# A Mamba and mixture-of-experts layer in fp32: another layout of the tile table, the last five blocks combined in tiles that lie idle, and an order of its own for the last post stage

## What is computed

```python
xz = einsum('bld,ed->ble', layernorm(x), in_proj_w);  x_ssm, z = split(xz, 2)
x_conv = silu(conv4(x_ssm) + conv_b)                  # causal, 4 taps
B, C, delta = split(einsum(x_conv, x_proj_w))         # 16, 16, 1 (softplus)
h = exp(delta * A) * h + delta * B * x_conv           # over time, 16 states
y = (sum_n(h * C) + D_param * x_conv) * silu(z)
x1 = x + einsum(y, out_proj_w)
top 2 of 8 experts by softmax(router(layernorm(x1))), weights w
out = x1 + sum_k w_k * (layernorm(x1) @ expert_weights[top_k])
```

## Time and profile before

| | us |
|---|---|
| median of 3 runs | 2971.43 |
| the runs | 2971.4 to 2974.65 |
| profiled execution | 2975.89 |
| its span, first to last instruction | 2974.1 |
| TensorE / VectorE / GpSimd / ScalarE busy | 2415.0 / 2278.7 / 1811.8 / 1486.8 |
| mean granted TensorE clock, share of full | 0.875 |

### The profile page before, as it was taken

How to read it: one execution, slowest core, us unless ns; L and a number is a source line. 1 busy time by engine, 2 the same in 40 slices (tenths; PEclk the granted TensorE clock), 3 DMA queues, 4 the chain that set the end, 5 groups by cost and what they waited for, 6 DMA issues and landing times.

```text
span 2974.1 us, 34543 instructions
## 1 busy us (share of the span) xinstructions
PE 2415.0 (81%) x9510; PEld 1401.4 (47%) x9510; DVE 2278.7 (77%) x3189; ACT 1486.8 (50%) x2417; POOL 1811.8 (61%) x1420
## 2 busy tenths in 40 slices
PE   5668686798979898898979898898979898887754
PEld 2335353455545554555545554545545554444421
DVE  3889888898888888888888898888888888665100
ACT  3454545465555556455655546465645556342210
POOL 2455766566566767576676767577675767574412
PEclk8778777798989999898989898899979898899977
DMA  3762411223233434334343434344343434455735
GB/s 123 243 244 92 142 54 57 85 86 117 72 113 105 144 103 125 116 108 141 108 122 106 139 111 133 105 119 130 115 126 98 150 103 131 124 161 157 192 97 129
DMA packets 192570, 366.27 MB, mean 123 GB/s; under 512 B 22912, under 2 KB 22912, under 8 KB 192384
## 3 DMA queue, kind: packets, MB, share of 16 engines
q1 hardware_dynamic: 144272, 263.26, 27.4%
q0 software_dynamic: 28672, 67.13, 10.6%
q10 hardware_dynamic: 19440, 33.69, 3.1%
HBM read 212.73 MB, written 151.26 MB: 122 GB/s over the span
## 4 chain that ended last, share of the span: by engine, by line
PE 47%; DVE 19%; issue 13%; ACT 7%; DMA 7%; POOL 6%; SPq 0%; DVEq 0%; POOLq 0%; ACTq 0%
PE work L1094 34%; DVE h L919 8%; PE hT L1099 7%; DVE acc L927 6%; PE work L1099 3%; POOL u L646 3%; DMA x_out<-result_scratch,rows_of 3%; PE work L1154 2%; ACT decay L783 2%; DVE xc L950 1%; DMA b_ring<-b_scratch 1%; DMA xe<-row_scratch 1%; ACT L783 1%; POOL x_out L750 1%; DMA result_scratch<-ye 1%
## 5 line engine op out<-in xcount | busy, mean ns | idle before, releaser
L646 POOL TENSOR_TENSOR u<-xc,b_ring 128x1024 f32<-128x1024 f32 x512 | 1229.8, 2411 | 757.2 <-DVE h L919 576.0
L783 ACT ACTIVATE decay<-dt,neg_a 128x512 f32<-128x512 f32 x1024 | 700.8, 689 | 690.1 <-DVE h L919 675.0
L1099 PE MATMUL hT<-ident,h 128*128 128x128 f32 x4096 | 693.4, 305 | 364.6 <-DVE acc L927 290.4
L1099 PEld LDWEIGHTS hT<-ident,h 128*128 128x128 f32 x4096 | 524.7, 156 | 650.3 <-DVE acc L927 285.5
L1094 PE MATMUL work<-w_exp,xeT 128*128 x1528 | 749.1, 636 | 37.4 <-DVE dt L962 13.6
L927 DVE SCALAR_TENSOR_TENSOR acc<-hT,ct,acc 128x512 f32<-128x512 f32 x960 | 699.8, 729 | 86.9 <-PE hT L1099 83.9
L919 DVE TENSOR_TENSOR_SCAN h<-decay,h_last,u 128x512 f32<-128x512 f32 x512 | 652.7, 1275 | 114.1 <-ACT decay L783 77.8
L919 DVE TENSOR_TENSOR_SCAN h<-decay,u 128x512 f32<-128x512 f32 x512 | 621.4, 1215 | 123.6 <-ACT decay L783 93.2
L1094 PE MATMUL work<-xnT,w_in 128*128 128x512 f32 x1024 | 484.2, 618 | 2.2 <-DVE dt L962 1.5
L1094 PEld LDWEIGHTS work<-w_exp,xeT 128*128 128x128 f32 x1528 | 295.5, 204 | 366.8 <-issue 366.1
L750 POOL DMA_INDIRECT x_out<-result_scratch,rows_of x120 | 192.7, 1606 | 184.9 <-DMA x_out<-x_scratch 91.0
(11 more groups left out here) (145 smaller groups left out, 1856.7 us busy)
## 6 DMA issues: line engine op xcount, KB each, us to landing
b_ring<-b_scratch SPq DMA_DIRECT2D x256, 256.0 KB
xe<-row_scratch SPq DMA_DIRECT2D x165, 256.0 KB
result_scratch<-ye SPq DMA_DIRECT2D x165, 256.0 KB
row_scratch<-x_out ACTq DMA_DIRECT2D x32, 1024.0 KB, 4.8
x<-in_x SPq DMA_DIRECT2D x66, 256.0 KB, 5.4
x_scratch<-x SPq DMA_DIRECT2D x64, 256.0 KB, 2.0
xn<-in_x SPq DMA_DIRECT2D x62, 256.0 KB, 3.4
x_out<-x_scratch SPq DMA_DIRECT2D x60, 256.0 KB, 3.1
```

The costliest lines, as they stand in the source:

```text
L646: nc.gpsimd.tensor_tensor(out=u[:, at:at + 2, :], in0=xc[:, half, 2 * k:2 * k + 2, :], in1=b_ring[:, n % ROWS:n % ROWS + 1, :].to_broadcas ...
L783: nc.scalar.activation(decay_bank[g % 2][:], dt[:, half, :], ACT.Exp, scale=neg_a[:, c, n:n + 1]).then_inc(decay_ready, 1)
L1099: last = nc.tensor.transpose(ps[:, k * P:(k + 1) * P], tile(k), ident[:])
```

## The change

Four things. The table of tiles lies with one tile per partition, its numbers in units of rows, which makes `new_group` 14 dependent operations instead of 19, each on few elements. Blocks 11 to 15 ("late", of = 0 to 4) are no longer combined through `x_out` but each in four tiles of its own, by then unused: in `xnT`, the two halves of `h`, `u` and `x1`; their first gathers are issued for all four quarters, then the second ones. Block 11 goes in stage 15, 12 and 13 in the last stage, 14 at the head of the closing tiles, 15 at the end. The results' scratch has three parts instead of two, and the table of group 7 is made at the end of stage 15 instead of in the last stage. The post stage of block 15 has an order of its own (`POST_END`), in which its four weighted first rows go into the idle `xc`. And all tables of places have new numbers, of which two lines are shown; `gate_weights` computes the mask of the ranks first.

```diff
-    COMBINE_PLAN = {j: [j - 5] for j in range(5, BLOCKS - 1)}
-    COMBINE_PLAN[BLOCKS - 1] = [BLOCKS - 6, BLOCKS - 5]
-    COMBINE_PLAN[BLOCKS] = [BLOCKS - 4, BLOCKS - 3]
-    COMBINE_PLAN[BLOCKS + 1] = [BLOCKS - 2]
-    COMBINE_PLAN[BLOCKS + 2] = [BLOCKS - 1]
-    NEW_GROUP = {first + n + 1: g for g, (first, n) in enumerate(GROUPS)}
+    COMBINE_PLAN = {j: j - 5 for j in range(5, BLOCKS)}
+    LATE = 5
+    NEW_GROUP = {first + n + 1: g for g, (first, n) in enumerate(GROUPS[:-2])}
...
-        "silu_z": [60.57],
+        "silu_z": [63.09],
...
-        "expert": [11.51, 14.24, 18.5, 27.8, 31.94, 35.21, 40.91, 44.16, 51.51, 56.71, 58.7, 61.45],
+        "expert": [12.95, 13.84, 18.76, 27.8, 33.76, 34.9, 40.91, 47.46, 52.88, 56.98, 59.44, 64.58],
...
+        if j == BLOCKS - 1:
+            steps += late_in("far", 0) + [(COMBINE_LATE["middle_new_group"][0], ("new_group", len(GROUPS) - 2))]
+        if j == BLOCKS:
+            steps += late_in("mid", 1) + late_in("near", 2)
...
         if j == BLOCKS + 2:
-            return ([("gather", q, 0) for q in range(Q)] + [("gather", q, 1) for q in range(Q)] + [("store", q) for q in range(Q)])
+            return late("late_gather", 4) + late("late_store", 4)
         count = EXPERT_PLAN[j][2]
-        tiles = [[("rows_load", 0), ("rows_load", 1), ("rows_T", 0), ("rows_load", 2), ("rows_evict", 0)]]
+        steps = [("new_group", len(GROUPS) - 1), ("rows_load", 0), ("rows_load", 1)] + late("late_fetch", 4) + late("late_fetch", 3) + late("late_gather", 3)
+        steps += [("rows_T", 0), ("rows_load", 2), ("rows_evict", 0)]
         for i in range(count):
...
-        rows = [[("fetch", q), ("gather", q, 0), ("gather", q, 1), ("store", q)] for q in range(Q)] + [[("fetch_last", q) for q in range(Q)]]
...
-            steps += rows[i // 3] if i % 3 == 0 and i // 3 < len(rows) else []
+            steps += late("late_store", 3) if i == count // 2 else []
...
+        def late_tile(of, q):
+            return (xnT[:, q, :], h[:, 0, q, :], h[:, 1, q, :], u[:, q, :], x1[:, q, :])[of]
+
+        def x_first_of(r, q):
+            return xc[:, 0, q, :] if r == BLOCKS - 1 else x_first[:]
...
+                        if k == 0:
+                            pool.wait_ge(late_loaded[of], 16 * Q)
                         else:
-                            pool.wait_ge(loaded, 16 * (BLOCKS + 1))
+                            pool.wait_ge(late_row[of * Q + q], 16)
...
-                        link(nc.vector.tensor_tensor(out=past, in0=tiles_to[0:1, :].rearrange("p (a e) -> p a e", a=1).to_broadcast([1, XT, E]),
-                                                     in1=tile_no[:].rearrange("p (i a) -> p i a", a=1).to_broadcast([1, XT, E]), op=ALU.is_le))
-                        link(nc.vector.tensor_reduce(expert_f[:], past, AX.X, ALU.add))
+                        link(nc.vector.tensor_scalar(past[:, 0, :], tiles_to[:], tile_at[:, 0:1], None, ALU.is_le))
+                        link(nc.vector.scalar_tensor_tensor(out=past[:, 1, :], in0=tiles_to[:], scalar=tile_at[:, 0:1], in1=tiles_f[:],
+                                                            op0=ALU.is_le, op1=ALU.mult))
+                        link(nc.vector.tensor_reduce(passed[:], past[:], AX.X, ALU.add))
```

More of the change, by code:

```diff
@@ L83, in mamba_moe_kernel @@
-        "gate_exp": [31.68],
-        "gate_sum": [30.88],
-        "gate_weights": [37.97],
-        "rank": [40.13],
-        "row_of": [40.34],
-        "weigh": [41.91, 46.9, 52.3, 57.15],
-        "scatter": [45.9, 48.02, 55.57, 61.9],
+        "load_res": [0, 4.56, 7.16, 13.35],
+        "y_T": [3.95, 4.16, 4.17, 4.17],
+        "y_skip": [5.28, 5.98, 8.38, 9.52],
+        "y_gate": [8.46, 11.27, 11.48, 11.76],
+        "out_project": [10.41, 12.16, 14.54, 16.54],
+        "residual": [14.16, 16.46, 17.58, 18.56],
@@ new lines, in mamba_moe_kernel @@
+        "rstd2": [19.44, 20.88],
+        "store_x1": [12.83, 15.36, 19.16, 19.72],
+        "norm2": [18.08, 18.74, 23.3, 24.11],
+        "norm2_T": [17.86, 18.75, 22.5, 25.68],
+        "norm2_evict": [18.84, 21.17, 25.24, 27.48],
+        "router": [18.55, 19.8, 25.56, 27.11],
+        "gate_logits": [18.75, 22.45, 27.07, 29.84],
+        "gate_top": [32.08],
+        "gate_exp": [34.84],
+        "gate_sum": [33.53],
+        "gate_weights": [37.11],
+        "rank": [39.92],
+        "row_of": [40.66],
@@ L139, in mamba_moe_kernel @@
     }
     PAIRS = [(i, k) for i in range(Q) for k in range(TOP)]
-    INDEX = {"gather": PAIRS, "conv": [(c, k) for c in range(C) for k in range(EDGE)]}
+    INDEX = {"gather": PAIRS, "late": [(i, k) for k in range(TOP) for i in range(Q)], "conv": [(c, k) for c in range(C) for k in range(EDGE)]}
     def steps_in(stage):
@@ L163, in experts_in, with late_in @@
                 for i, at in enumerate(places) if i < EXPERT_PLAN[j][2]]
-    def combine_in(j):
-        blocks = len(COMBINE_PLAN.get(j, []))
-        return [((at + i * N * C) / blocks, (kind, i * Q + s[0]) + tuple(s[1:])) for i in range(blocks) for at, (kind, *s) in steps_in(COMBINE)]
+    def late_in(kind, of):
+        places = COMBINE_LATE[kind + "_fetch"], COMBINE_LATE[kind + "_gather"], COMBINE_LATE[kind + "_store"]
+        return ([(at, ("late_fetch", of, q)) for q, at in enumerate(places[0])] +
+                [(at, ("late_gather", of) + index) for index, at in zip(INDEX["late"], places[1])] +
+                [(at, ("late_store", of, q)) for q, at in enumerate(places[2])])
@@ L179, in closing_steps @@
-        for i, tile in enumerate(tiles):
-            steps += tile
-            steps += rows[i // 3] if i % 3 == 0 and i // 3 < len(rows) else []
+            steps += [("rows_T", i + 1)] * (i + 1 < count) + [("rows_load", i + 3)] * (i + 3 < count)
+            steps += [("rows_evict", i + 1)] * (i + 1 < count) + [("expert", i), ("expert_evict", i), ("rows_store", i)]
+            steps += late("late_store", 3) if i == count // 2 else []
         return steps
@@ L579, in steps_of @@
                     elif s[0] == "store":
[L580 removed]
+                        block, q = COMBINE_PLAN[j], s[1]
                         first = block * T + q * P
[L582 to L587 removed]
+                        sync.wait_ge(gathered[q % 2], 16 * TOP * (2 * block + q // 2 + 1))
@@ L1056, in steps_of @@
-                        if g >= 3:
-                            for k in range(2):
-                                dve.wait_ge(gathered[k], 16 * TOP * Q // 2 * GROUPS[g - 2][0])
-                        link(nc.vector.tensor_copy(rows_of[g % 3][:], result_f[:]))
+                        link(nc.vector.tensor_reduce(result_f[:], token_shift[:], AX.X, ALU.add))
+                        wait_combined(dve, g - 3)
+                        link(nc.vector.tensor_tensor(out=rows_of[g % 3][:], in0=result_f[:], in1=row_f32[:], op=ALU.add))
@@ L1084, in _ @@
         def _(pe):
-            pe.wait_ge(const_step, 16)
+            pe.wait_ge(const_step, 14)
             def take(j, key):
```

322 lines of the change are left out of this document (184 added, 138 removed).

## The result

The changed kernel takes 2882.96 us, the median of four runs (2881.6 to 2892.7), against 2971.41 (2970.8 to 2974.7). The ratio is 0.9694, 95% interval 0.9668 to 0.972, a change of -88.5 us. The forecast was 2881 in 2845 to 2915. The sum was met; two of its terms were met by what offset inside them, as the rest shows.

What follows compares the result with a forecast made beforehand. The prediction looked first at what keeps TensorE waiting in the 272 us tail, then at the scan stages. Terms -47 - 26 - 4 - 13 + 17 - 17 = -90 us gave 2886 against the profiled 2975.9, 2881 for the median, range 2845 to 2915.

Steps and rivals of the forecast that it cites:

- Closing tiles, -47: Closing tiles after the last stage: no store waits among the tile loads any more, 70 us against 117.1.
- the last of the forecast's rivals: Closing tiles: closing gathers slow the tile loads, so TensorE waits as often as before; near 2925 us, chance 0.02.
- Last stage, -26: Last stage, up to the landing of the last scatter and the first closing load: four savings, sum -25.7 us.
- (a): Last stage: group 7's table is made at the end of stage 15, so TensorE's 10.3 us first-tile wait goes.
- (c): End of last stage: the last `weigh` waits for no scatter, no gather stands among the scatters; 4.2 against 6, -1.8 us.
- (d): Last stage to closing tiles: the tile load waits for scatters alone, -7.9 us.
- (b): Last stage: about five of nine TensorE eviction waits go (3.7 us), and the clock is not lowered (about 2 us).
- The third rival: Last stage gets no shorter: a `weigh` waiting for gate weights holds up evictions; 17.8 us given back, 2899, chance 0.10.
- Table, -13: Table in scan stages 3 to 15: 14 operations, 3.1 us instead of 5.0; -1.85 in each of seven stages, wholly on path.
- Seam, +17: Between scan stages: silu behind the last decay, late product after odd stages; +14 odd, +3 even, bounds 0 and +45.
- Rest of the scan stages, -17: Scan stages: 9 us from VectorE's waits for `u`, 8 from the ranks, nothing from the residual; bounds -60 and +40.
- The first rival: Scan stages gain more: half of VectorE's 43.9 us residual wait goes, seam costs nothing; 2842 us, chance 0.15.

## Why the forecast was right, and where it wasn't

**Closing tiles, -47:** -49.7 measured, and +50 when the order is put back. No wait there is over 6.3 us, so the gathers did not slow the loads as the last of the forecast's rivals had it. The fetch burst that was costed at 3 us costs 1.0, and the gathers' 2 don't show. But this is cover, not a low price: with an earlier start the burst costs 5.2 us and the low clock behind it. The forecast took bytes over a rate; the load waits for a queue of issues and transfers in front of it (the issues of the eight fetches alone take 3.7 us).

**Last stage, -26:** -20.5. (a) 10.3: 9.5 by the medians and 10.2 by the traces came back in its experiment, with a table that is 1.7 us shorter. (c) 1.8: from the last product at 2779.88 to the last scatter's end at 2784.33 are 4.45 us, forecast 4.2. (d) 7.9: from the last scatter's issue to the first load are 3.6 us instead of 13.5, 9.9. (b), 3.7 and 2, failed: the eviction waits stayed, and TensorE is busy 94.4 us for 93.2. I had counted places where other transposes stand ahead of the product; in the last tiles nothing but its own do, and it waits 0.88 us for their eviction, where it waited 0.93 and 0.97 before. Hence the last scatter is issued 106.6 us behind the last scan and not 98. The third rival (nothing of (a) to (c)) is refuted: the first weigh step waits 0.74 us for the gate weights. It is the other way round: the later weigh steps stand behind evictions, up to 2780, and an early place for them brought the last scatter forward by 12.5 us.

**Table, -13:** -1.65 each instead of -1.85, seven times -11.6. TensorE's wait shows all of it, as said; the stage lengths of its experiment do so in their sum alone.

**Seam, +17:** the waits at place 0 grew by 41 us in stages 3 to 14 and those at place 61 went (-20): +21. The size was nearly right. The step that failed is the sentence that this part "speaks against the change": with the silu back the kernel is 23 us slower, and with the product back none faster.

**Rest of the scan stages, -17:** the table takes 9.9 of the 14.4 us in stages 3 to 14, so seam and rest together gave -4.5 in the profiles (forecast 0), and -11.6 by the run with the old places. In these stages that run differs from the kernel before by the table, the order of the mask's operations and the results' scratch in three parts with its waits, yet gained 2.8 us where the table gives 9.9; how much of this is one execution's scatter stays open. Inside the term most steps failed: the `u` waits rose by 35 us instead of falling by 9. Only 5.3 of their 14.4 us stood behind a seam, at place 4, where the forecast's reason applies, and these went; at places 38 and 54 they grew from 9 to 47 us. That the later places of B rows and gathers did this is argued, no run moves them alone; the residual's 43.9 us, taken as nothing, went. The ranks' came as said (18.1 to 8.1 with the fill's, forecast -8). What the new numbers visibly bring is TensorE's clock at places 28 to 48, for which the forecast had no term, though the trace before shows it (0.90 in stage 9).

**The first rival** (scan stages gain 39 more) is refuted, and so are the second and the fourth: the seam cost 21 us, not 45 or 112.

So the total was met in part by luck: the closing tiles, the table and the seam's size came as computed, while in the last stage a term that failed was met by one that gave more, and in the scan stages the rest came to near its number by other ways than those named.

## What to carry to other kernels

On an in-order queue what counts is what the transfers ahead of a needed one wait for and how many they are: put stores where their gathers have long landed, and spread fetches one per tile, clear of the gathers, instead of four or eight in a row. A wait that goes is only worth what the engine behind it can't take back; read the stage's length, not the wait. When a table of places is renumbered, compare TensorE's busy time for the same matmuls, and its granted clock, first: they tell at once whether the clock moved.

## What the runs showed of the hardware

TensorE needed 1726.8 us before and 1696.9 after for the same 7068 matmuls of stages 3 to 14 (0.91 and 0.93 granted). In stage 9 the clock fell in a wait of 1.0 us that followed waits of 1.9 and 1.3 us, and a product behind it took 6.49 us instead of 3.69; in the changed kernel's stretch with waits of 1.2, 1.1 and at most 0.8 us it did not fall. The rows of a tile load of 256 KB are used 2.9 us after its issue when little stands before it, 5.5 behind eight fetches and 9.0 behind four with gathers beside them; with gathers beside it alone it lands after 6.2. And with the places untouched a scan stage takes 1.5 to 5 us more in some executions (stage 15 with a clock of 0.86 for 0.89): a change of 5 us in this kernel can't be told by one profile.
